# Recurrent mixer: turned inverse blocks loaded by ScalarE between its last gate tanhs, the other inverse blocks by SyncE behind their store

## The reference

```
mixed = silu(conv1d(hidden_states @ W_qkv.T, conv_w))        # 4 taps, per channel
q, k, v = split(mixed);  z = hidden_states @ W_z.T;  g, beta = gates(hidden_states)
def step(Sst, inp):                                          # one position t
    Sst = Sst * exp(g_t)[..., None, None]
    kv = einsum('bhkv,bhk->bhv', Sst, k_t)
    delta = (v_t - kv) * b_t[..., None]
    Sst = Sst + k_t[..., None] * delta[..., None, :]
    o = einsum('bhkv,bhk->bhv', Sst, q_t)
h_ = o * silu(z)
out = (h_ * rsqrt(mean(h_ * h_) + eps) * norm_weight) @ W_out.T
```

## Time and profile before

| | |
|---|---|
| median of three runs | 3156.9 us (3155.66 to 3166.07) |
| the profiled execution's own time | 3159.19 us |
| its span in the profile | 3157.5 us |
| granted TensorE clock, mean of the span | 0.877 of full speed |
| the recurrent mixer's turns with a solve | 16, from about 1000 to 2200 us |

### The profile page before, as it was taken

One profiled execution on the slowest core, in us unless ns is written; L12 is line 12 of the kernel. 1 busy time (PEld: TensorE's weight loads), 2 busy tenths in 40 slices (PEclk: granted clock), 3 DMA queues, 4 the chain that ended last, 5 costly groups with the idle time before them and its releaser, 6 DMA issues. The chain is left out here.

```text
span 3157.5 us, 53822 instructions
## 1 busy us (share of the span) xinstructions
PE 2447.2 (78%) x19384; PEld 1877.8 (59%) x19384; DVE 2088.9 (66%) x5024; ACT 1247.4 (40%) x2999; POOL 809.4 (26%) x646
## 2 busy tenths in 40 slices
PE   6888886997455888888888888876543756689798
PEld 5666664886444666666667666655332644466554
DVE  4777773332338888888888888875454336687573
ACT  0434342221145666665666666643000213344132
POOL 1111100000113332233222222231287125550110
PEclk9999997998578999999999999988665887889799
DMA  5220001001212221111112211111211762110000
GB/s 138 64 67 12 12 9 52 21 24 29 87 64 51 52 52 46 49 48 49 44 48 49 51 49 48 45 44 29 74 51 24 227 198 56 47 52 10 18 24 24
DMA packets 277730, 168.94 MB, mean 54 GB/s; under 512 B 186303, under 2 KB 253702, under 8 KB 277112
## 3 DMA queue, kind: packets, MB, share of 16 engines
q1 hardware_dynamic: 251333, 140.22, 15.8%
q0 software_dynamic: 26112, 25.03, 3.0%
HBM read 99.17 MB, written 73.45 MB: 55 GB/s over the span
## 5 line engine op out<-in xcount | busy, mean ns | idle before, releaser
L1149 POOL TENSOR_TENSOR qd<-decay,qm 114x456 f32<-114x456 f32 x128 | 143.7, 1145 | 651.2 <-DVE qm L1242 499.2
L1563 PE MATMUL d_ps<-d_xT,w_qkv 128*128 128x228 f32 x1024 | 235.0, 389 | 48.3 <-DVE qmask L1357 28.9
L1563 PEld LDWEIGHTS d_ps<-d_xT,w_qkv 128*128 128x128 f32 x1024 | 215.4, 212 | 79.5 <-issue 42.0
L2216 POOL DMA_INDIRECT s_eo<-rows_y,slots_all x128 | 152.5, 1191 | 148.5 <-POOLq L87 110.5
L1210 DVE TENSOR_TENSOR elim_tmp<-ue 128x30 f32<-128x30 f32 (+14 forms) x480 | 179.3, 374 | 13.8
L463 PE MATMUL t_ps<-xT,w_qk 128*128 128x154 f32 x1024 | 150.9, 300 | 40.4 <-DVE qk L300 31.0
L1212 DVE TENSOR_TENSOR ue<-ue,elim_tmp 128x30 f32<-128x30 f32 (+14 forms) x480 | 170.4, 355 | 16.5
L1284 DVE SCALAR_TENSOR_TENSOR y_v<-raw,taps,y_v 128x228 f32<-128x228 f32 x384 | 161.2, 493 | 14.3 <-ACT y_v L1414 14.2
L463 PEld LDWEIGHTS t_ps<-xT,w_qk 128*128 128x128 f32 x1024 | 136.7, 189 | 52.0 <-DVE qk L300 38.2
L1551 PE MATMUL d_ps<-gl,after 114*114 114x456 f32 x256 | 132.7, 637 | 41.0 <-DVE sz L1297 41.0
L1376 ACT ACTIVATE decay<-d_ps,gates 114x114 f32<-114x114 f32 x512 | 133.4, 371 | 65.4 <-PE d_ps L1551 65.0
(11 more groups left out here) (337 smaller groups left out, 5656.9 us busy)
## 6 DMA issues: line engine op xcount, KB each, us to landing
rows_x<-zero_row SPq DMA_DIRECT2D x4, 2048.0 KB, 7.8
ue<-blocks_n SPq DMA_DIRECT2D x16, 512.0 KB, 4.7
blocks_u<-ue SPq DMA_DIRECT2D x16, 512.0 KB, 2.7
blocks_v<-on SPq DMA_DIRECT2D x16, 512.0 KB, 2.8
e_x<-rows_x SPq DMA_DIRECT2D x32, 256.0 KB, 4.2
e_gu<-L_ffn_w_gate_up SPq DMA_DIRECT2D x32, 256.0 KB, 4.2
rows_y<-e_y SPq DMA_DIRECT2D x32, 256.0 KB, 3.3
blocks_n<-nt SPq DMA_DIRECT2D x96, 64.0 KB
```

What stands on the lines that cost most here:

```text
L1149: pool.tensor_tensor(qd[p.par][s][:, hs(u), :].rearrange("p (a o b) t -> p a o b t", o=2, b=2)[:, :, o], e[o][:, :, :].rearrange("p (a b) ...
L1563: last = pe.matmul(ps[:, f % 2, (t % 2) * W:(t % 2 + 1) * W], w_qkv[:, k, t * 128:(t + 1) * 128], xT[:, k, :], start=(k == 0), stop=(k == ...
L2216: pool.indirect_dma_start(out=eo[n % 2][:, s * TOPK + k, :], out_offset=None, in_=rows_y, in_offset=bass.IndirectOffsetOnAxis(ap=slots_all ...
```

## The change

SyncE no longer waits for the turned store, and no longer issues the four loads of turned blocks. Its eight loads of the other blocks follow both stores and the wait for their own store. ScalarE gets a new function `turned_load`, called between gate tanh 2 and gate tanh 3: it waits for the turned store and for the clearing of `upd`, and issues the same four transfers to the same semaphore. One semaphore is added for bookkeeping. Nothing that is computed changes, and no size of a transfer.

```diff
@@ block.sync, iteration @@
                         sp.dma_start(ud.rearrange("s h q c i -> (s h q) (c i)"), ue[:, :, :].rearrange("p c i -> p (c i)")).then_inc(ud_out, 16)
                         sp.wait_ge(uet_r, r.n + 1)
                         sp.dma_start(vd.rearrange("s h q i c -> (s h q) (i c)"), uet[:, :]).then_inc(vd_out, 16)
-                        sp.wait_ge(vd_out, r.n * 16 + 16)
-                        sp.sem_inc(sp_gate, 1)
-                        sp.wait_ge(x_clear, r.n * 2 + 2)
-                        sp.sem_inc(sp_gate, 1)
-                        for s in range(2):
-                            for rows, _, o in JOINS:
-                                sp.dma_start(x[s][rows, :, o:o + BW], vd[s, :, o // 16].rearrange("h i c -> i h c")).then_inc(u_in, 16)
                         sp.wait_ge(ud_out, r.n * 16 + 16)
                         sp.sem_inc(sp_gate, 1)
                         need(sp, t_mm, r.n * 8)
@@ block.scalar @@
+                def turned_load(r):
+
+                    act.wait_ge(vd_out, r.n * 16 + 16)
+                    act.sem_inc(act_gate, 1)
+                    act.wait_ge(x_clear, r.n * 2 + 2)
+                    act.sem_inc(act_gate, 1)
+                    for s in range(2):
+                        for rows, _, o in JOINS:
+                            act.dma_start(x[s][rows, :, o:o + BW], vd[s, :, o // 16].rearrange("h i c -> i h c")).then_inc(u_in, 16)
+
@@ block.scalar, iteration @@
                     exps(3)
                     if z:
                         gate_tanh(r, 2)
+                        turned_load(r)
                         gate_tanh(r, 3)
```

More of the change, by code:

```diff
@@ L1016, in delta_net @@
          kq_mm, qm_r, gl_r, dec_mm, e_r, nt_r, qd_r, sel_r, elim_r, z_mm, thz_r, sz_r, vt_mm, p_mm, rc_r, t_mm, xc_r,
-         o_mm, og_r, osq_r, ms_r, rms_r, on_r, ot_mm, oT_r, wo_mm, h_r, d_dve, pe_gate, pool_gate, sp_gate, x_clear,
+         o_mm, og_r, osq_r, ms_r, rms_r, on_r, ot_mm, oT_r, wo_mm, h_r, d_dve, pe_gate, pool_gate, sp_gate, act_gate, x_clear,
          uet_r, vd_out, u_in, zz_mm, zs_r, ww_mm, wr_r, x_gap) = (
@@ L1023, in delta_net @@
                 "thz_ready", "sz_ready", "vt_mm", "p_mm", "rhs_ready", "t_mm", "x_ready", "o_mm", "og_ready", "osq_ready",
-                "ms_ready", "rms_ready", "on_ready", "ot_mm", "oT_ready", "wo_mm", "h_ready", "dve", "pe_gate", "pool_gate", "sp_gate", "x_cleared",
+                "ms_ready", "rms_ready", "on_ready", "ot_mm", "oT_ready", "wo_mm", "h_ready", "dve", "pe_gate", "pool_gate", "sp_gate", "act_gate", "x_cleared",
                 "inverse_turned", "turned_out", "turned_in", "join1_mm", "join1_ready", "join2_mm", "join2_ready", "x_gap_cleared"))
```

## The result

The changed kernel takes 3181.7 us (median of six runs, 3171.96 to 3190.99) against 3157.1 for the kernel before on the same chip (3155.66 to 3166.07). The ratio is 1.0071, with a 95% interval of 1.0046 to 1.0095: about 22 us slower. Forecast were 3163 and the range 3144 to 3184. The time lies inside the range, near its upper end; the forecast loss of 6 us was too small by a factor of about four.

A forecast was written before the change was run, and what follows sets the result against it. VectorE, 86% busy in the mixer's turns, was taken as the bound. Late joins +21, tap wait -14 and last two turns -1 gave +6 us: 3163, range 3144 to 3184.

The forecast's parts named there:

- the signs named ahead: Timeline marks: four ScalarE issues within 2 us, 1.5 us or more before tanh 3, join wait about 40, tap wait near 0.
- the forecast's own 3153 to 3174: Range of the main forecast alone, without rivals: mixer join late by 1.0 to 2.0 us a turn; chance 0.40.
- (a): Turned loads on ScalarE between gate tanhs: four issues take about 2 us, gate tanh 3 starts 0.4 to 0.9 us late.
- (c): Two load streams share DMA engines, at most 1/0.82 = 1.22 of one stream's load: turned blocks late by 1.2 us.
- (d): Earlier inverse blocks end TensorE's 3.09 us wait at the second product; VectorE's conv tap wait goes: -14 us.
- (f): SyncE reaches its later issues (blocks, inputs, residual) 2 to 3 us earlier; no VectorE wait goes back to them: 0.
- (e): Last two mixer turns, without a conv beside them: gain of 0 to 1.2 us each, taken as -1 for both.
- (b): SyncE's inverse-block loads start just after their own store lands, 3.5 us earlier, ahead of or beside the turned loads.
- Undisturbed streams: Rival: the two load streams don't disturb each other, join late by only 0.4 us, time 3146; chance 0.27.
- the paragraph behind the sum: Remark that believing a second queue carries the turned blocks free would omit +1.5 us a turn and give 3146.
- Exclusive issues: Rival: only one engine's loads are issued at a time, ScalarE's four take 3.8 us, tanh 3 2.3 late, 3174; chance 0.23.
- The third rival: TensorE's second product waits for late instructions, not blocks, so the tap wait stays: +21 us, 3178; chance 0.10.

The follow-up runs named there:

- e8: Changed kernel, but SyncE starts its eight ut loads only after ScalarE has issued its last turned load; 3170.90 us, ratio 1.0020 to the kernel before.
- e1: Changed kernel, but SyncE issues the ut loads only when the turned blocks have landed; 3192.21 us, ratio 1.0093 to the kernel before.
- the repeat: The changed kernel measured once more, unaltered, in later rounds; 3200.00 us against 3164.05 for the kernel before, ratio 1.0104.
- e4: Changed kernel, but SyncE holds its later transfers (inputs, residual, ue) until TensorE's second product is done; 3176.59 us, ratio 1.0040 to the kernel before.
- e3: Changed kernel, but GpSimd's two masks of ue wait until VectorE has finished the next pair's conv; 3167.97 us, ratio 1.0026 to the kernel before.
- e6: Kernel before, with SyncE issuing three ut loads, then the four turned loads, then the other five; 3164.02 us, ratio 1.0000.
- e2: Changed kernel, but SyncE issues all loads, eight ut loads first and the turned ones behind, ScalarE none; 3205.19 us, ratio 1.0137 to the kernel before.
- e9: Changed kernel, but ScalarE issues the turned loads behind gate tanh 3 instead of ahead of it; 3208.58 us, ratio 1.0138 to the kernel before.

## Why the prediction was right, and where not

The stated range holds the time, and the signs named ahead came: four issues within 2 us (1.99), 1.87 us before gate tanh 3, 36.7 us of waiting for the join, 1.5 for the tap. But that the time falls into the range is luck in part. Its upper end was made of a join 2.6 us late, measured is 1.3; two losses that stood in no term or at 0, of 8.6 and 8.9 us, fill the room between. The time lies outside the forecast's own 3153 to 3174.

The sum against the kernel before, from the 14 turns and the rows above:

| term of the prediction | forecast | measured |
|---|---|---|
| join read starts late, (a) to (c) | 14 x 1.5 = +21 | 14 x 1.32 = +18.5 |
| join read longer | none | 14 x 0.61 = +8.6 |
| wait for the tap, (d) | -14 | 1.5 - 14.2 = -12.7 |
| conv steps beside the masks, (f) | 0 | (166.0 + 146.3) - (142.2 + 161.2) = +8.9 |
| last two turns, (e) | -1 | +2.3 for the first; the last lies behind the stretch |
| the rest | | +2.1, of it +1.6 for decays |
| sum | +6 | +27.7 |

The conv term stands on these rows of the page, over all turns, after and then before:

```profile
L1277 DVE SCALAR_TENSOR_TENSOR y_qk<-raw,taps,y_qk 128x228 f32<-128x228 f32 x384 | 166.0, 507 | 23.3 <-ACT y_qk L1407 22.9
L1277 DVE SCALAR_TENSOR_TENSOR y_v<-raw,taps,y_v 128x228 f32<-128x228 f32 x384 | 146.3, 451 | 1.5 <-ACT y_v L1407 1.5
```

```profile
L1284 DVE SCALAR_TENSOR_TENSOR y_v<-raw,taps,y_v 128x228 f32<-128x228 f32 x384 | 161.2, 493 | 14.3 <-ACT y_v L1414 14.2
L1284 DVE SCALAR_TENSOR_TENSOR y_qk<-raw,taps,y_qk 128x228 f32<-128x228 f32 x384 | 142.2, 450 | 22.1 <-ACT y_qk L1414 21.7
```

**(a) and (b), right.** The first `ut` load went from 6.45 to 2.85 after the store, 3.6 earlier (forecast 3.5), and ScalarE issues its four in 1.99 us. Its sequencer runs on while the tanh executes. Tanh 3 is 0.83 late, at the upper of the two estimates, although the issues don't wait for the tanh's end. In the turn at 1736 they begin 0.1 us later behind its start than I had counted, take 0.1 longer, and leave 0.18 between their end and tanh 3.

**(c), about right in size, wrong in its ground.** Forecast was 1.2 us for the two streams' company. The median landing of a turned load says 0.8 (2.9 less 2.1). In the turn at 1736 the join product starts 4.90 us after the first turned issue, 1.2 more than the 3.7 of the earlier trace rows. In the means it is 0.87 (4.90 less 4.03), of which e8 and e1 give back 0.7. But the reason that I gave, a ceiling of 1/0.82, isn't one. The two streams together reached shares of 1.38 and 1.27 in the two microseconds before the join (length, PE, PEld, DVE, ACT and POOL busy, clock, DMA share, GB/s):

```profile
1743.00:1744.00 1.00, 0.14 (x3) 0.02 (x1) 0.69 (x1) 1.00 (x5) 0.00 (x0) 1.00 1.38 214
1744.00:1745.00 1.00, 0.63 (x4) 0.39 (x4) 0.00 (x0) 1.00 (x5) 0.00 (x0) 1.00 1.27 179
```

and moved up to 214 GB/s, where one stream moved 134 at 0.82. The share adds up overlapping packets and doesn't end at 1. Company costs less than I worked out from it.

**(d), right in itself**: 12.7 of the 14.2 us came, and 9.3 in the repeat (4.9 left). TensorE's granted clock stays at 1.00 from 1748 to 1754 us, beside and behind the second product of the turn at 1736; in the turn of the earlier trace rows it was 0.50 behind it. But the sum took the wait for the tap as pure gain, and part of the masks had run in it.

**(e), wrong in sign in the turn where it can be read whole.** In the turn at 2138 us the join read starts 1.37 later than in its counterpart of before (9.95 against 8.58). Nothing is given back there: the turn takes 67.30 us instead of 64.99. The last turn, from its store of the inverse to its last store of `hid`, takes 55.06 us instead of 56.35. The two together are +1.0 instead of -1.

**(f), the step that failed.** I priced the earlier transfers at 0, since VectorE's list of waits had no entry that goes back to them. That list can't show this cost: it is not a wait but longer instructions, +8.9 us. The `ue` load is issued at 11.51 after the store instead of 15.75, GpSimd masks the blocks as soon as they land, and does so beside `y_qk`. The load's place isn't what costs: in e4 it is at 18.86, the masks are beside `y_v`, and VectorE loses 25.1 us to them. What costs is that VectorE no longer stands still beside them, by (d)'s own gain. The row that would have warned me was in the page: `y_v` steps took 493 ns and `y_qk` steps of the same shape 450. Asked why, I would have found the masks beside the slow ones. The Trainium skill says in "SBUF — State Buffer", section "SBUF: two separate sides", that VectorE with two inputs in SBUF and a GpSimd instruction that reads SBUF exclude each other over a shared pair of ports. The trace agrees: one conv step stands still for each mask (1.49 and 1.44 us instead of 0.44), and a mask can be held for long while the steps beside it run at full speed. In e4 the one that starts at 1593.55 us took 9.08 us, and the 16 conv steps that start beside it up to 1599.1 took 0.45 each. So the masks' own length doesn't tell what VectorE loses: GpSimd's first mask took 5.2 us on average before, 1.8 in the changed kernel, 3.3 in its repeat and 1.3 alone in e3, while VectorE lost 15.5, 23.6, 24.9 and nothing in its conv steps.

**The missing term.** That the join could also get longer, by TensorE's waits for its own instructions in every second turn, stood in no step. Such waits stood in the trace of before (7.0 us in all for L1627). e4 shows that they grow with the transfers beside the join, and the `instruction` queue's packet, which starts later there, is the likely path; it is argued from the order in time. Which transfer delays it stays open.

**The rivals.** Undisturbed streams (3146) fell by the timeline and by e1 and e8. (With the whole +1.5 a turn left out, as the paragraph behind the sum has it, the time would be 3142; 3146 keeps 0.4 a turn.) Exclusive issues (3174) came nearest to the time, and for the wrong reason: the four issues took 1.99 us, not 3.8, beside SyncE's eight in 4.18. The Trainium skill's rule of an exclusive lock during an issue ("Perfetto Trace Analysis", section "DMA Instruction — HWDGE (DVE, Sync)") isn't seen here over the length of an issue: one on ScalarE takes a median of 510 ns beside SyncE's and 510 alone in e8. SyncE's own for `ut` went from 418 to 487 ns. The third rival fell with the tap wait, but its ground was half right: TensorE's second product waits 13.0 us on "issue" now, in 14 places, against 8.6 in 6 before.

## What to carry to other kernels

When transfers are moved forward, price not only who waits for them but what work they release and whose instructions it will then run beside; two groups of the same operation and shape with different mean times (493 and 450 ns here) show where such a neighbour already costs. Before a wait is counted as gain, look what runs in it: here GpSimd's masks did, and 8.9 us of the 12.7 went back to them. Loads that end together with another chain on the critical path should get no company: here a second issuing engine delayed the data by 0.8 us. And price the order too, since with three of `ut` ahead of the turned loads SyncE alone lost nothing (e6), with eight ahead 1.4% (e2). And a gain can be hidden behind a second one: the split loads alone gave 0, the late masks alone 0.23%, both 0.40%, though the last two intervals overlap.

## What the runs showed of the hardware

- ScalarE begins to issue DMAs 0.30 us after its activation of 0.60 us has started in ten of the 16 turns (0.15 to 0.75 in the others), and its four issues take about 2 us beside another issuer or alone (1.93 to 2.40 in the 16 turns of the changed kernel, 1.93 to 2.10 in e8, where SyncE is silent). Behind gate tanh 3, in one turn of e9, four took 3.27 us.
- A load on ScalarE's queue and one on SyncE's cost each issuer about the same: medians of 510 ns for L1430 (309 to 916) and 487 for L1094 (318 to 1775). A load of turned blocks lands a median of 2.1 us after its issue alone (before, e1, e8) and 2.9 beside SyncE's in the changed kernel.
- GpSimd's two masks over 128x1024 values, 1.27 and 1.50 us, lengthened 24 conv steps of VectorE from 8.89 to 10.92 us: one step by 1.0 us for each mask. Where VectorE stood waiting, a mask cost it nearly nothing (0.72 us for the longest step in the turn at 1477).
- TensorE's waits at the join that the profile puts down to "issue" went from 7.0 to 13.4 us between 1030 and 2110 us with no change in TensorE's own program. Each ends 1.2 to 1.6 us after a packet of 16 KB on the queue `instruction`.
